# Turning a gate chain's rows between the halves of a step's scores in an mLSTM mixer

## The chip, the cores and the metric

The kernel runs on one core of one Trainium2 chip. The metric is device microseconds of one execution; the time before is the median of three runs.

## The reference, cut to what matters

A decoder block on x of shape (8, 256, 256): a Mamba layer with its MLP, an mLSTM cross mixer, and a feed-forward network with fp4 rounding. The change touches the mixer alone. Its part of the reference, for each batch b of 8 and each of 4 heads (width 64):

```python
log_fg = jax.nn.log_sigmoid(fg)
cs = jnp.cumsum(log_fg, axis=2)
log_D = cs - cs_shift.T + ig.T            # lower triangle, else -inf
max_log_D = jnp.max(log_D, axis=-1, keepdims=True)
D = jnp.exp(log_D - max_log_D)
qk = einsum(q, k) / sqrt(64)
C = qk * D
normaliser = maximum(abs(sum(C)), exp(-max_log_D))
h = einsum(C / (normaliser + 1e-8), v)
h_norm = (h - mean(h)) / sqrt(var(h) + 1e-5) * (1 + out_w)
```

The kernel writes log_D as a(t) minus a running maximum R(s), with a = ig minus the running sum of log_fg. It needs for each token a (the exponent's bias) and exp(-(cs + R)), called nm, which bounds the normaliser. It also needs R as a row, cut into three bf16 pieces that add up to it.

## The kernel before, in words

The mixer and the feed-forward network stand in one block, one program for each engine. A program is a list of stages with a lag: in step s a stage with lag g works on batch s minus g (`pipelines`, L144, and `step`, L151 onwards). Steps 0 to 11 of the mixer are written out; from step 7 on the first stages of the feed-forward network stand beside them. The order within a step is the order of the list, and each engine runs its instructions in that order. `only(n, stage)` puts a stage into step n alone.

- **TensorE**, a step: `scores1_even`, `scores0`, `scores1_odd` of batch s-1 (L1608: the products of keys and queries; keys of the second chunk with even heads, keys of the first chunk, keys of the second chunk with odd heads), then `sums` of batch s-2 (L1636 to L1638: weights times values), then `args` of batch s (L1591 to L1600: the exponents' arguments from R's pieces).
- **ScalarE**: `exps` of batch s (L1720), `squares` of batch s-2 (L1727).
- **VectorE**: `weights` of batch s-1 in two parts (L1784: scores times exponentials), `variance` of batch s-3 (L1813), `normalise` of batch s-2 (L1795 to L1806), `scale` of batch s-3 (L1818). `normalise` raises `h_read`.
- **GpSimd**: `rstds` of batch s-3 (L1878, L1880: the reciprocal root), then `residual` (L1885, L1888).
- **SyncE** loads rows of R (`load_r`, L91) and keys (`load_k`, L1567) for batches 2 to 7 in turn.

The gates' chain (`GateChain`) runs twice, for 16 rows (4 batches of 4 heads) each. The second half's runs inside the mixer's steps, one piece at a time, since batches 4 to 7 need it only from step 4 on. Its places before the change:

- step 2, VectorE, at the end: `maxima` (L399 to L411): the running maximum, then first piece, remainder, second piece, remainder, third piece, and nm's exponent cs + R. SyncE then stores the pieces (L455), and reads them back for batch 4.
- step 3, TensorE, after all of `scores`: `turn_a` (L442), two transposes of a into bank 6. VectorE, at the start of step 3: `a_tokens` (L415) copies them out and raises `gates_done` to 1.
- step 4, ScalarE, at the start: `exp_nm` (L427). TensorE, after all of `scores`: `turn_nm` (L449), into bank 7. VectorE, at the start: `nm_tokens` (L419) copies them out and raises `gates_done` to 2.

Banks 6 and 7 are the ones that `sums` writes, so the turned rows must be copied out before `sums` goes on: `sums` of batch 1 (step 3) waits for `gates_done` at 1, `sums` of batch 2 (step 4) at 2. `turn_a` waits for `h_read` of batch 0, `turn_nm` for that of batch 1, since both overwrite sums that `normalise` reads.

Of the kernel before, what the change touches and what calls it, by code (L numbers as in the profile page):

```python
# [357 lines left out]
class GateChain:  # L358
# [37 lines left out]
    def maxima(self, dve):  # L396
        at = self.SUMS_AT
        dve.wait_ge(self.dve, at)
        dve.tensor_tensor_scan(self.R, self.aT, self.aT, -3e38, ALU.max, ALU.max).then_inc(self.dve, 1)  # L399
        dve.wait_ge(self.dve, at + 1)  # L400
        dve.tensor_copy(self.pieces[:, 0, :], self.R).then_inc(self.dve, 1)
        dve.wait_ge(self.dve, at + 2)
        dve.tensor_tensor(self.rest[:, 0, :], self.R, self.pieces[:, 0, :], ALU.subtract).then_inc(self.dve, 1)
        dve.wait_ge(self.dve, at + 3)
        dve.tensor_copy(self.pieces[:, 1, :], self.rest[:, 0, :]).then_inc(self.dve, 1)
        dve.wait_ge(self.dve, at + 4)
        dve.tensor_tensor(self.rest[:, 1, :], self.rest[:, 0, :], self.pieces[:, 1, :], ALU.subtract)\
           .then_inc(self.dve, 1)
        dve.wait_ge(self.dve, at + 5)
        dve.tensor_copy(self.pieces[:, 2, :], self.rest[:, 1, :]).then_inc(self.dve, 1)  # L410
        dve.tensor_tensor(self.nm, self.cs, self.R, ALU.add).then_inc(self.dve, 1)  # L411
# [80 lines left out]
def on(stage, unit, *args, n=B):  # L492

    if 0 <= unit < n:
        stage(unit, *args)


def front(m):
# [91 lines left out]
    chain = GateChain(m, 0, lambda name, shape: (over_dead_bc if shape[0] == P else over_dead_x)(name, shape))  # L590
# [641 lines left out]
    def _(dve):  # L1232
# [50 lines left out]
        def soft_start():  # L1283
            dve.wait_ge(s["dt_ps"], 4)
            dve.tensor_tensor(raw.rearrange("p (t h) -> p t h", h=NH),
                              bank[7][:, 0:W].rearrange("p (t h) -> p t h", h=NH),
                              middle(m.head_c[:, 0, :], T), ALU.add).then_inc(s["cs_step"], 1)
            dve.wait_ge(s["cs_step"], 1)
            softplus_start(dve, s["sp_dve"], raw, work, 1.0)

        def soft_rest():
            n = softplus_finish(dve, s["sp_dve"], s["sp_act"], flat(m.dt[:]), work, 1.0)
            dve.wait_ge(s["sp_exp"], 1)
            dve.tensor_scalar(neg_a[:], neg_a[:], -1.0, None, ALU.mult).then_inc(s["sp_dve"], 1)
            dve.wait_ge(s["sp_dve"], n + 1)
            dve.tensor_tensor(m.da[:], m.dt[:], middle(neg_a[:], T), ALU.mult).then_inc(s["da_ready"], 1)

        def pieces_of_sums():
            at = 1

            def step(ins):
                nonlocal at
                at += 1
                ins.then_inc(s["cs_step"], 1)
                dve.wait_ge(s["cs_step"], at)

            turned = bank[7][:, 3 * P:4 * P]
            shifted, grid, below = work[0], work[1], work[2]
            dve.wait_ge(s["da_ps"], 1)
            dve.wait_ge(s["filled"], 1)  # L1310
            step(dve.tensor_scalar(shifted, turned, FLOOR, ON_GRID, ALU.max, ALU.add))
            step(dve.tensor_scalar(grid, shifted, ON_GRID, None, ALU.subtract))
            step(dve.scalar_tensor_tensor(below, turned, FLOOR, grid, ALU.max, ALU.subtract))
            dve.tensor_tensor_scan(both[:, 0, :], ones, grid, 0.0, ALU.mult, ALU.add)
            step(dve.tensor_tensor_scan(both[:, 1, :], ones, below, 0.0, ALU.mult, ALU.add))
            step(dve.tensor_copy(pieces[:, :, 0, :], both))
            step(dve.tensor_tensor(rest, both, pieces[:, :, 0, :], ALU.subtract))
            step(dve.tensor_copy(pieces[:, :, 1, :], rest))
            step(dve.tensor_tensor(rest, rest, pieces[:, :, 1, :], ALU.subtract))
            dve.tensor_copy(pieces[:, :, 2, :], rest).then_inc(s["pieces_ready"], 1)  # L1320
# [83 lines left out]
        def ctx_last():  # L1404
            dve.wait_ge(g["ctx_last"], 1)
            dve.wait_ge(s["later_in"], 16 * len(LATER))
            dve.tensor_tensor(m.graw[:, C * CTX_SUMS:, :], bank[7][:, 0:C * 2 * XH].rearrange("p (c g) -> p c g", c=C),
                              middle(m.gate_b[:], C), ALU.add).then_inc(g["last_saved"], 1)
# [20 lines left out]
        def quantise(b, first, end):  # L1429
            if first == 0:  # L1430
                dve.wait_ge(g["ffn_w_in"], 16)
                after(dve, g["wq_step"], Quantiser.STEPS * b)
            for k in range(first, end):
                wq.step(k, b, m.ffn_w[:, b * UNIT:(b + 1) * UNIT])

        for k in range(STEPS):
            b = k - SCAN
            on(sums, b - 3)
            if k == 6:
                soft_start()  # L1440
            on(apply, 2 * k - 2)
            on(apply, 2 * k - 1)
            on(convolve, k - 2, [0, 1])
            if k == 6:
                soft_rest()
            on(convolve, k - 2, [2, 3])
            if k == 7:
                pieces_of_sums()
            on(convolve, k - 2, [4])
            on(stats, 2 * k)  # L1450
            on(stats, 2 * k + 1)
            units = UNITS.get(k, [])
            two = len(units) == 2
            on(hidden, k - MLP, 0)
            if units:
                quantise(units[0], 0, 5 if two else 3)
            on(center_sum, 2 * (k - MLP - 2))
            on(center_sum, 2 * (k - MLP - 2) + 1)
            on(hidden, k - MLP, 1)
            on(center, 2 * (k - MLP - 2))  # L1460
            on(center, 2 * (k - MLP - 2) + 1)
            if units:
                quantise(units[0], 5 if two else 3, 9 if two else 5)
            on(inputs, b)
            on(outputs, b - 1, 0)
            on(weights, b, 0)
            on(outputs, b - 1, 1)
            on(weights, b, 1)
            if b == 4:
                ctx_last()  # L1470
            on(hidden, k - MLP, 2)
            if units:
                quantise(units[-1], 0 if two else 5, 5 if two else 7)
            on(hidden, k - MLP, 3)
            if units:
                quantise(units[-1], 5 if two else 7, 9)
            if k == MLP + 7:
                chain.logs(dve)
            on(residual, k - MLP - 1)
            if k == MLP + 7:  # L1480
                chain.sums(dve, *FIRST_HALF)
            on(gate_rows, k - MLP - 3)
            on(norm, k - MLP - 1)
            if k == MLP + 6:
                dve.wait_ge(g["gates_saved"], B // 2)
                chain.start(dve)
            if k == MLP + 7:
                chain.maxima(dve)
            if k == MLP + 8:
                chain.a_tokens(dve, TOKENS[0])  # L1490
                chain.nm_tokens(dve, TOKENS[1])
                dve.tensor_scalar(m.out_w[:], m.out_w[:], 1.0, None, ALU.add)
# [3 lines left out]
def mixer_and_ffn(m):  # L1496
# [24 lines left out]
    chain = GateChain(m, 1, lambda name, shape: sb(name, shape)[:])  # L1521
# [3 lines left out]
    for kk in range(KF):  # L1525
        w = min(P, FF - kk * P)
        at = GU_ROWS * D + kk * P
        down_groups.append(([m.ffn_w[:, at + i * FF:at + i * FF + w] for i in range(KD)], m.w_dn[0:w, kk, :]))
    saved_all = m.gu_saves + KF
    only = lambda step, stage: (lambda b, p: stage() if b == step else None, 0)  # L1530
# [54 lines left out]
    def _(pe):  # L1585
# [109 lines left out]
        def turn_nm():  # L1695
            pe.wait_ge(s["h_read"], LEAD + 2)
            chain.turn_nm(pe, TOKENS[1])

        mixer = [(scores1_even, 1), (scores0, 1), (scores1_odd, 1), only(3, turn_a), only(4, turn_nm), (sums, 2),
                 (args, 0), only(1, lambda: chain.turn_logs(pe, *SECOND_HALF))]  # L1700
        forward = [(turn_x, 2), (lambda t, p: turn_down(0 if t == 0 else 2) if round_at(t) and t < 2 else None, 2),
                   (turn_h, 4), (gate_up, 2), (lambda t, p: turn_down(1) if round_at(t) and t == 0 else None, 2),
# [4 lines left out]
    def _(act):  # L1707
# [58 lines left out]
                dst = down_groups[2 * n + half][1]  # L1766
                act.activation(dst, bank[5][0:dst.shape[0], half * D:(half + 1) * D], ACT.Copy).then_inc(m.w_saved, 1)

        mixer = [only(0, lambda: chain.exp_logs(act)), only(4, lambda: chain.exp_nm(act)), (exps, 0), (squares, 2)]
        forward = [(turned_x, 2), (lambda t, p: save_down(0 if t == 0 else 2) if round_at(t) and t < 2 else None, 2),  # L1770
                   (turned_h, 4), (lift_x, 1), (lift_h, 3), (silu, 2),
                   (lambda t, p: save_down(1) if round_at(t) and t == 0 else None, 2), (norm, 0)]
# [3 lines left out]
    def _(dve):  # L1776
# [76 lines left out]
        def output(t, p):  # L1853
# [8 lines left out]
        chain.start(dve)  # L1862
        chain.logs(dve)
        mixer = [only(3, lambda: chain.a_tokens(dve, TOKENS[0]).then_inc(m.gates_done, 1)),
                 only(4, lambda: chain.nm_tokens(dve, TOKENS[1]).then_inc(m.gates_done, 1)),
                 (lambda b, p: weights(b, p, 0), 1), (lambda b, p: weights(b, p, 1), 1), (variance, 3),
                 only(1, lambda: chain.sums(dve, *SECOND_HALF)), (normalise, 2),
# [93 lines left out]
```

## Time and profile before

| | us |
|---|---|
| median of three runs (603.13 to 605.93) | 604.32 |
| the profiled execution's own time | 606.77 |
| its span, first to last instruction | 605.1 |
| TensorE busy | 567.9 (94%) |
| VectorE busy | 446.4 (74%) |
| ScalarE busy | 270.1 (45%) |
| GpSimd busy | 144.6 (24%) |
| mean granted TensorE clock | 0.966 |

How to read it: one execution was profiled, and its times run from the first instruction. The mixer's block begins near 389.8 us; its step 3 is the stretch from about 401.7 us, step 4 from about 412.5 us, step 5 from about 419.8 us. TensorE's granted clock is given as a share of 2.4 GHz: 1.00 is 2.4 GHz, 0.50 is 1.2 GHz. PE is TensorE's matmuls, PEld its weight loads, DVE VectorE, ACT ScalarE, POOL GpSimd, SPq the issue of a DMA by SyncE. An f32 matmul shows as two records.

### The profile page before, as it was taken

Reading aid. Unit: us, or ns where it says so; the run is one execution under the profiler, and the core shown is the slowest. Engines: PE = TensorE matmul, PEld = TensorE weight load, DVE = VectorE, ACT = ScalarE, POOL = GpSimd, SP = SyncE. Lnnn points to the kernel's source line nnn. Section 1 sums busy time; section 2 is a strip of 40 time slices with the busy share of each in tenths; the row PEclk is TensorE's granted clock in tenths of the full one; section 3 lists DMA queues with packets and bytes.
Section 4 is the critical chain, followed back from the end, with each engine's and each line's share of the span. In section 5 each row is a group of like instructions: output and inputs, shape, how many; then the busy total and the mean of one; then the engine's idle time right before and its main releaser. Section 6 shows DMA issues by size and latency. Waiting matters only on the chain. (4 is left out here: it accounts for less than half of the span.)

```text
span 605.1 us, 9377 instructions
## 1 busy us (share of the span) xinstructions
PE 567.9 (94%) x2995; PEld 459.4 (76%) x2995; DVE 446.4 (74%) x990; ACT 270.1 (45%) x565; POOL 144.6 (24%) x209
## 2 busy tenths in 40 slices
PE   7989998999999899999999999989959899999995
PEld 6766666788888788888888888877855577777774
DVE  6986598379888324755655857575788999999994
ACT  2655877785788422222111112434434444444431
POOL 4120001134545021210110010005775222122200
PEclk8989999799999999999999999998977999999999
DMA  8300101000000093000000000011100000000000
GB/s 301 121 1 18 35 15 39 22 25 5 6 7 0 2 298 90 1 1 0 1 1 1 1 0 1 4 43 33 35 2 0 2 17 17 14 12 17 18 19 26
DMA packets 21392, 18.90 MB, mean 31 GB/s; under 512 B 12008, under 2 KB 20584, under 8 KB 20968
## 3 DMA queue, kind: packets, MB, share of 16 engines
q1 hardware_dynamic: 20920, 18.36, 9.5%
q8 instruction: 22, 0.36, 0.3%
q14 instruction: 18, 0.15, 0.1%
q10 hardware_dynamic: 432, 0.03, 0.1%
HBM read 16.04 MB, written 2.34 MB: 30 GB/s over the span
## 5 line engine op out<-in xcount | busy, mean ns | idle before, releaser
L923 PE MATMUL ps<-xnT,w_fc 128*128 128x256 f32 x512 | 112.8, 380 | 0.0
L923 PEld LDWEIGHTS ps<-xnT,w_fc 128*128 128x128 f32 x512 | 96.5, 190 | 12.7
L1658 PE MATMUL ps<-w_fc,scores 128*128 128x352 f32 x256 | 82.3, 476 | 1.5 <-ACT scores L1747 1.5
L1658 PEld LDWEIGHTS ps<-w_fc,scores 128*128 128x128 f32 x256 | 48.9, 196 | 29.0 <-ACT scores L1747 3.6
L1166 ACT ACTIVATE xs<-ps 128x512 f32<-128x512 f32 x32 | 19.1, 597 | 95.8 <-PE ps L923 75.7
L1279 DVE SCALAR_TENSOR_TENSOR fold<-xpad,conv_w,fold 128x256 f32<-128x256 f32 x120 | 50.9, 481 | 2.4 <-ACT fold L1068 1.6
L1677 PE MATMUL ps<-u_res,hT 128*128 128x256 f32 x192 | 44.2, 380 | 3.8 <-DVE scores L1856 2.8
L1677 PEld LDWEIGHTS ps<-u_res,hT 128*128 128x128 f32 x192 | 36.3, 190 | 11.3 <-issue 3.0
L806 PE MATMUL ps<-xnT,fold 128*128 128x256 f32 x160 | 39.2, 393 | 1.6 <-ACT xpad L1062 0.8
L806 PEld LDWEIGHTS ps<-xnT,fold 128*128 128x128 f32 x160 | 30.7, 198 | 9.5 <-issue 3.6
L813 PE MATMUL ps<-fold,xnT 128*128 128x512 f32 x64 | 36.8, 708 | 0.0
L732 POOL TENSOR_SCALAR q_ve<-q_mv 128x2 f32<-128x2 f32 x8 | 1.7, 217 | 129.3 <-DVE q_mv L1393 129.3
L898 PE MATMUL ps<-w_out,xF 128*128 128x256 f32 x128 | 30.4, 381 | 1.5 <-DVE u_res L1368 1.5
L1377 DVE TENSOR_TENSOR fold<-ps,xs 128x512 f32<-128x512 f32 x16 | 11.1, 691 | 26.2 <-ACT xs L1166 26.2
L898 PEld LDWEIGHTS ps<-w_out,xF 128*128 128x128 f32 x128 | 23.7, 190 | 8.1 <-issue 5.5
L714 POOL TENSOR_TENSOR bc<-xs,head_c 128x512 f32<-128x512 f32 x16 | 24.1, 1507 | 20.7 <-DVE zs L1361 20.7
L936 PE MATMUL ps<-zs,xpad 128*128 128x256 f32 x128 | 28.4, 380 | 0.0
L936 PE MATMUL ps<-zs,fold 128*128 128x256 f32 x128 | 28.3, 379 | 0.0
L936 PEld LDWEIGHTS ps<-zs,fold 128*128 128x128 f32 x128 | 24.3, 190 | 3.3
L936 PEld LDWEIGHTS ps<-zs,xpad 128*128 128x128 f32 x128 | 24.2, 190 | 3.3
L1377 DVE TENSOR_TENSOR xpad<-ps,xs 128x512 f32<-128x512 f32 x16 | 11.1, 692 | 20.2 <-ACT xs L1166 20.2
L1385 DVE TENSOR_TENSOR x_res<-x_res,ps 128x256 f32<-128x256 f32 x16 | 6.7, 419 | 24.2 <-PE ps L936 24.2
(299 smaller groups left out, 1208.8 us busy)
## 6 DMA issues: line engine op xcount, KB each, us to landing
zs<-in_ffn_w SPq DMA_DIRECT2D x1, 2112.0 KB, 10.9
x_res<-in_x SPq DMA_DIRECT2D x8, 256.0 KB, 7.6
w_fc<-in_w_fc SPq DMA_DIRECT2D x1, 2048.0 KB, 10.3
xnT<-in_ctxT SPq DMA_DIRECT2D x8, 256.0 KB, 3.1
xs<-in_ctx SPq DMA_DIRECT2D x16, 128.0 KB, 3.0
xs<-in_ctxT SPq DMA_DIRECT2D x8, 256.0 KB, 3.1
out<-scores SPq DMA_DIRECT2D x16, 128.0 KB, 1.7
fold<-in_w_in SPq DMA_DIRECT2D x2, 580.0 KB, 6.6
```

The lines of the kernel that those rows point to most:

```text
L714: pool.tensor_tensor(heads(dx[:, c, :]), heads(m.xs[:, n, :]), inner(m.head_c[:, 2, :], HD), ALU.mult)\
L806: last = pe.matmul(bank[1 + n % 2][:, 0:S], w_in[:, kk, w0:w0 + P], turned_u(b, kk), start=(kk == 0), stop=(kk == KD - 1))
L813: last = pe.matmul(bank[3 + c][:], turned_u(b, kk)[:, c * P:(c + 1) * P], w_in[:, kk, 0:DI], start=(kk == 0), stop=(kk == KD - 1))
L898: last = pe.matmul(bank[6][:, c * D:(c + 1) * D], ygT[:, c, k * P:(k + 1) * P], m.w_out[:, k, :], start=(k == 0), stop=(k == DI // P - 1))
L923: last = pe.matmul(bank[half + r][:, i * S:(i + 1) * S], m.w_fc1[:, kk, col:col + P], m.xnT[:, b, kk * S:(kk + 1) * S], start=(kk == 0), s ...
L936: last = pe.matmul(bank[4 + c][:, 0:D], hid[p][:, k, c * P:(c + 1) * P], w_fc2[:, k, :], start=(k == 0), stop=(k == KM - 1))
L1166: act.activation(gate[:, r, :], bank[2 + r][:], ACT.Silu).then_inc(g["gate_ready"], 1)
L1279: dve.scalar_tensor_tensor(conv[:, p, k, :], xpad[:, p, k, tap:tap + S], m.conv_w[:, ch, tap:tap + 1], conv[:, p, k, :], ALU.mult, ALU.add)\
L1377: dve.tensor_tensor(hid[p][:, 2 * pair:2 * pair + 2, :].rearrange("p k t -> p (k t)"), bank[r][:], gate[:, r, :], ALU.mult).then_inc(g["hi ...
L1385: dve.tensor_tensor(m.x_res[:, n, :], m.x_res[:, n, :], bank[4 + c][:, 0:D], ALU.add)\
L1658: last = pe.matmul(bank[1 + j][:, 0:HALF], xT[:, p, k * P:(k + 1) * P], m.w_gu[:, k, j * HALF:(j + 1) * HALF], start=(k == 0), stop=(k == ...
L1677: last = pe.matmul(bank[7][:, 0:D], hT[:, p, k, :], m.w_dn[:, k, :], start=(k == 0), stop=(k == KF - 1))
```

## The change

TensorE's two turns move ahead of `scores1_odd` of their step. `maxima` is cut after the first remainder: what follows (second piece, remainder, third piece, nm's exponent) becomes `maxima_rest`. In the second half's chain `maxima_rest` stands in step 3, right behind `a_tokens`; in the first half's it is called right behind `maxima`, as before. ScalarE's `exp_nm` moves from the start of step 4 to the start of step 3, ahead of `exps` of batch 3. No instruction is added or removed, and no wait gets another value.

```diff
@@ -401,6 +401,9 @@
         dve.tensor_copy(self.pieces[:, 0, :], self.R).then_inc(self.dve, 1)
         dve.wait_ge(self.dve, at + 2)
         dve.tensor_tensor(self.rest[:, 0, :], self.R, self.pieces[:, 0, :], ALU.subtract).then_inc(self.dve, 1)
+
+    def maxima_rest(self, dve):
+        at = self.SUMS_AT
         dve.wait_ge(self.dve, at + 3)
         dve.tensor_copy(self.pieces[:, 1, :], self.rest[:, 0, :]).then_inc(self.dve, 1)
         dve.wait_ge(self.dve, at + 4)
@@ -1486,6 +1489,7 @@
             if k == MLP + 7:
                 chain.maxima(dve)
+                chain.maxima_rest(dve)
@@ -1696,7 +1700,7 @@
-        mixer = [(scores1_even, 1), (scores0, 1), (scores1_odd, 1), only(3, turn_a), only(4, turn_nm), (sums, 2),
+        mixer = [(scores1_even, 1), (scores0, 1), only(3, turn_a), only(4, turn_nm), (scores1_odd, 1), (sums, 2),
                  (args, 0), only(1, lambda: chain.turn_logs(pe, *SECOND_HALF))]
@@ -1766,7 +1770,7 @@
-        mixer = [only(0, lambda: chain.exp_logs(act)), only(4, lambda: chain.exp_nm(act)), (exps, 0), (squares, 2)]
+        mixer = [only(0, lambda: chain.exp_logs(act)), only(3, lambda: chain.exp_nm(act)), (exps, 0), (squares, 2)]
@@ -1862,6 +1866,7 @@
         mixer = [only(3, lambda: chain.a_tokens(dve, TOKENS[0]).then_inc(m.gates_done, 1)),
+                 only(3, lambda: chain.maxima_rest(dve)),
                  only(4, lambda: chain.nm_tokens(dve, TOKENS[1]).then_inc(m.gates_done, 1)),
```

## Rows read from the trace of the kernel before

**Rows 1.** Chain of work that ended last, 384 to 458 us: start us, us, what

```profile
405.03 0.18 DVE a_tok L415
...
414.91 0.25 ACT nm L427
```

**Rows 2.** Windows: stretch, us, busy PE PEld DVE ACT POOL, granted clock, DMA, GB/s

```profile
405.35:412.50 7.15, 7.15 (x32) 5.77 (x32) 4.16 (x11) 0.71 (x2) 1.84 (x2) 0.52 0.16 43
412.50:415.94 3.44, 2.37 (x20) 2.08 (x19) 0.47 (x3) 2.65 (x9) 2.54 (x2) 1.00 0.01 2
...
419.80:442.60 22.80, 22.80 (x182) 20.22 (x181) 17.78 (x42) 12.31 (x36) 16.98 (x17) 1.00 0.09 25
442.60:454.00 11.40, 4.93 (x31) 4.32 (x30) 9.21 (x25) 3.15 (x7) 7.70 (x10) 0.68 0.01 2
```

**Rows 3.** Timeline of TensorE, steps 3 to 5: start, us, instruction, [idle before <-releaser]

```profile
401.72 2.13 PE L1608 MATMUL ps<-xnT,xs 64*128 64x128 f32 x16
403.78 0.29 PE L442 MATMUL ps<-ident,aT 16*128 16x16 f32 x2
405.35 0.41 PE L1636 MATMUL ps<-xs,zs 128*128 128x65 f32 x2 [1.28 <-DVE a_tok L415]
...
412.46 2.13 PE L1608 MATMUL ps<-xnT,xs 64*128 64x128 f32 x16
415.29 0.27 PE L449 MATMUL ps<-ident,nm 16*128 16x16 f32 x2 [0.70 <-ACT nm L427]
415.94 0.41 PE L1636 MATMUL ps<-xs,zs 128*128 128x65 f32 x2 [0.38 <-DVE nm_tok L419]
...
419.81 2.13 PE L1608 MATMUL ps<-xnT,xs 64*128 64x128 f32 x16
```

**Rows 4.** Timeline from 403.24 us: weight loads at the end of the scores

```profile
403.24 0.41 PEld L1608 LDWEIGHTS ps<-xnT,xs 64*128 64x128 f32 x3
```

**Rows 5.** Timeline of VectorE, steps 2 and 3

```profile
400.74 0.17 DVE L1795 TENSOR_SCALAR den<-ps 128x8 f32<-128x8 f32 x1 [1.38 <-PE ps L1638]
...
401.58 0.76 DVE L1806 TENSOR_TENSOR scores<-ps,den 128x256 f32<-128x256 f32 x2
...
403.27 0.41 DVE L403 TENSOR_TENSOR max_rest<-R,max_parts 16x256 f32<-16x256 f32 x1
403.72 0.28 DVE L405 CAST max_parts<-max_rest 16x256 bf16<-16x256 f32 x1
...
404.69 0.41 DVE L411 TENSOR_TENSOR nm<-cs,R 16x256 f32<-16x256 f32 x1
405.03 0.17 DVE L415 COPY a_tok<-ps 128x32 f32<-128x32 f32 x1
...
406.92 0.66 DVE L1813 TENSOR_REDUCE var<-scores 128x8 f32<-128x512 f32 x1
...
411.95 0.68 DVE L1818 TENSOR_TENSOR scores<-scores,rv 128x512 f32<-128x512 f32 x1
```

**Rows 6.** Timeline of ScalarE

```profile
403.90 0.68 ACT L1727 ACTIVATE scores<-scores 128x512 f32<-128x512 f32 x1
...
414.75 0.40 ACT L427 ACTIVATE nm<-nm 16x256 f32<-16x256 f32 x1
```

**Rows 7.** Timeline of GpSimd

```profile
408.09 1.64 POOL L1880 TENSOR_TENSOR rv<-var,minus_half 128x8 f32<-128x8 f32 x1
```

**Rows 8.** Timeline of SyncE's queue, and a DMA issue (KB, us to landing)

```profile
404.79 0.32 SPq L455 DMA_DIRECT2D running_max<-max_parts  x1
...
406.56 0.55 SPq L1567 DMA_DIRECT2D xs<-in_ctxT  x1
...
xs<-in_ctxT SPq DMA_DIRECT2D x6, 256.0 KB, 3.1
```

**Rows 9.** Timeline of TensorE: the network's first two tiles

```profile
454.14 8.03 PE L1658 MATMUL ps<-w_fc,scores 128*128 128x352 f32 x16 [1.49 <-ACT scores L1747]
...
464.33 5.00 PE L1658 MATMUL ps<-w_fc,scores 128*128 128x352 f32 x16
```

## The prediction

> **What bounds the kernel now.** The change moves work of steps 3 and 4 of the mixer, so I read those steps engine by engine. TensorE's timeline says what a step should cost: from the start of step 5's scores on, TensorE is busy without a gap, 22.80 of 22.80 us at a granted clock of 1.00 (2.4 GHz) [rows 2]. There TensorE sets the pace. Steps 3 and 4 are different. Step 3 runs from 401.72 to 412.46 (10.74 us), step 4 from 412.46 to 419.81 (7.35 us) [rows 3]. The reader is to see three things in them.
>
> First, TensorE stands idle for 1.28 us until a_tok is copied out, and only then begins batch 1's sums at 405.35 [rows 3]. The copy was late for no reason of its own: a was turned by 403.78 + 0.29 = 404.07, but VectorE was inside `maxima` until nm's exponent, started 404.69, and came to a_tok at 405.03 [rows 3, 5]. The chain that ended last passes through it [rows 1]. Second, right after that gap the granted clock falls: 0.52 on average from 405.35 to 412.50 [rows 2], that is 1.2 GHz for nearly all of it, with TensorE busy throughout. Third, in step 4 turn_nm waits 0.70 us for ScalarE's exponential of nm, which stands behind batch 3's `exps`, and the sums wait another 0.38 us for nm_tok [rows 1, 3].
>
> **The change part by part.** I follow the new order from 401.72, where nothing has changed yet.
>
> *a turned between the halves.* The last four records of the scores are the odd half. Their first weight load stands at 403.24 and the turn followed at 403.78 [rows 3, 4], so the odd half with the switch into it is about 0.45 to 0.5 us. The turn can start at about 403.3 and be done at 403.6. `h_read` of batch 0 is no hindrance: normalise starts at 400.74 and the maxima behind it are already at 403.27 [rows 5].
>
> *a copied amid the maximum's pieces.* VectorE finishes the first remainder at 403.27 + 0.41 = 403.68 [rows 5]. The copy then runs from about 403.7 to 403.9 (0.17 us for a_tok [rows 5]). From a_tok's start to the first sum it took 405.35 - 405.03 = 0.32 us [rows 3, 5], so TensorE may go on at about 404.05. It is busy with the odd half until then: 403.3, 0.29 for the turn, 0.45 for the half, so 404.1. Batch 1's sums start at 404.1 instead of 405.35: **1.25 us** saved. The bounds are 1.0 (the turn costs TensorE two switches instead of one) and 1.4.
>
> *What stands behind the copy.* The four remaining instructions of `maxima` took 405.03 - 403.72 = 1.31 us [rows 5]; behind the copy they run from about 403.85 to 405.2, against 405.10 before. So the store of the pieces goes out some 0.1 to 0.15 us later than 404.79 [rows 8], and the rows and keys of batch 4 behind it in SyncE's queue likewise: keys issued at 406.7, landed 3.1 us later at 409.8 [rows 8]. They are first read by step 5's scores, in my sum at 414.6; this costs nothing as long as that cover of 4.8 us stands. `weights` of batch 2 come at most 0.1 us later, then variance: from 406.92 to about 407.0, ended at 407.65 [rows 5].
>
> *The clock.* From 405.35 to 412.46 TensorE did batch 1's sums and batch 3's args in 7.11 us. The same two stages one step later took 419.81 - 415.94 = 3.87 us at full clock [rows 3]. The gap ahead of them is gone, so I take the clock as held: **3.2 us** saved (7.11 - 3.9), and scores of batch 3 start at 404.1 + 3.9 = 408.0 instead of 412.46. They need weights of batch 2, which are over when variance starts at 407.0, so 1 us of cover is left. Bounds of this term: 0 if it falls all the same, 3.2 if not. I take the upper end, because the stretch nearest to the new one, steps 5 to 8, holds 1.00 over 22.80 us with the same stages back to back [rows 2].
>
> *nm's exponential one step up.* nm's exponent is there at about 405.25; ScalarE ends the squares of batch 0 at 403.90 + 0.68 = 404.58 [rows 6] and then waits for it some 0.7 us, with batch 3's `exps` queued behind. Those need args of batch 3, the last part of the stretch from 404.1 to 408.0, so not before some 407. The exponential (0.40 us [rows 6]) is over at 405.7, so nothing waits for ScalarE: cost nothing, with over 1 us of cover. The 0.70 us wait of turn_nm goes.
>
> *What is late next.* turn_nm would start at 408.0 + 1.6 = 409.6, the odd half end at 410.3 to 410.35. VectorE's nm_tokens stands behind `scale` of batch 0, and this becomes a wait that before did not have. Normalise of batch 1 starts at about 407.6, now straight after variance, and takes 1.6 us (400.74 to 401.58 + 0.76 in batch 0 [rows 5]), until 409.2. GpSimd's root started 1.17 us after variance started (406.92 to 408.09) and took 1.64 us [rows 5, 7]; with variance at 407.0 it is ready at 409.8. So `scale` starts at 409.8, 0.6 us after normalise; before, it started at 411.95, long after the root was there (409.73). nm_tok follows about 0.6 us later at 410.4, and the sums 0.34 us after that as in 415.94 [rows 3], at 410.7. TensorE stands for about 0.4 us. From the start of scores to that of sums step 4 then takes 2.7 us instead of 415.94 - 412.46 = 3.48 [rows 3]: **0.75 us** saved. Bounds: 0.4 (GpSimd or VectorE half as late again) to 1.1 (no stall).
>
> *Sum.* 1.25 + 3.2 + 0.75 = 5.2 us: scores of batch 4 start near 414.6 instead of 419.81. From there TensorE sets the pace again, `residual` of batch 0 is over before batch 2's sums are, and the rest of the mixer shifts as a whole. The way from the mixer into the network runs over VectorE and GpSimd, whose order is unchanged, so the shift reaches the end. Nothing changes ahead of 403 us: the first half's instructions keep their order. Against the profiled execution's own 606.77 this gives 601.6. That execution lies 2.45 us above the median of 604.32, so I take the difference off the median: **599.1 us**.
>
> **A rule of the skill beside the row.** The granted clock was 1.00 through the 0.70 and 0.38 us gaps of step 4 and fell after the 1.28 us one [rows 2, 3]. The Trainium skill (TensorE: Matmul & The Clock Gate, What's actually happening) says that activity releases the throttle and that the same kernel shows different numbers of cold matmuls from run to run. By that rule the 3.2 us would not be in every execution before, so not surely in the median; the trace, one execution, cannot show it. It is the first rival.
>
> **The rivals.**
>
> 1. *The stall goes, the clock term does not.* Either the timed executions before mostly kept 2.4 GHz through step 3, or after the change the clock falls at another place, such as the new 0.4 us wait. For it: the three runs spread over 2.8 us, nearly the 3.2 of the term, and the profiled one is above them all. Against it: 0.52 right behind the longest gap of these steps. Gain 1.25 + 0.75 = 2.0: 602.3.
>
> 2. *More than one fall saved.* If in timed executions the step 4 gaps (0.70 + 0.38 us) also bring the clock down, both falls go, 5.2 + 3.2 = 8.4 at most: 596.0 at the lowest, some 597.5 if it holds in half of them. Against it: in this trace it did not fall there.
>
> 3. *Slower: the network's first tiles stay at 1.2 GHz.* TensorE waits at the hand-over (4.93 us busy of 11.40, clock 0.68), and the first tile's 16 products took 8.03 us against 5.00 for the second [rows 2, 9]. The change moves these waits by 5 us in time. If the clock then comes back later, each further tile costs 3.0 us; from the second further one on the gain of 5.2 is gone: 599.1 + 6 = 605.1, with a third 608.1. Against it: TensorE was back up before the second tile, and VectorE is the busier of the two at the hand-over (9.21 us of 11.40 [rows 2]), which hides part of each 3 us.
>
> 4. *It does not do what it says*: the chain behind nm_tok is longer than I think (`scale` held by GpSimd, say by 1 us more), so step 4 gains nothing. Then 1.25 + 3.2 = 4.45, less up to 0.5: about 600.2. The direction stays.
>
> **How the numbers follow.** Forecast 0.56, rival 1 0.24, rival 2 0.06, rival 3 0.04, rival 4 0.10. The range takes in the forecast's own bounds (sum of the lower bounds 1.0 + 3.2 + 0.4 = 4.6, of the upper 5.7: 598.6 to 599.7), rivals 1 and 4, and about 1 us by which medians of such runs differ: 597.2 to 602.8. About 0.5% (3.0 us) is what a measurement of this kernel can tell from no change. Below 601.3 lie the forecast, rivals 2 and 4 and little of rival 1: faster 0.74. Rival 1 and the mild end of rival 3: same 0.23. Slower 0.03.
>
> **What would show it.** In the profile of the changed kernel: no wait of L1636 for a_tok over 0.2 us; a clock of 1.00 over steps 3 and 4; the nm exponential directly behind the first squares; no wait of L449 for ScalarE; a wait of L1818 for GpSimd of about 0.6 us in step 3 and of L1636 for nm_tok of about 0.4 us; 12.9 us from the scores of batch 2 to those of batch 4 instead of 18.1. The prediction is wrong if the clock falls in step 3 or 4 all the same, if the timed runs before were mostly without the fall, or if the hand-over to the network takes longer than before.

## The result, and the profile after

The changed kernel takes 599.65 us (median of 13 runs, 597.5 to 602.84) against 605.64 us (13 runs, 602.42 to 608.96) for the kernel before: ratio 0.9926, 95% interval 0.99 to 0.9951, so 3.0 to 6.1 us faster. The ratio is not that of the two medians, which would be 0.9901: it gives 4.5 us, they give 6.0. The profiled execution took 597.5 us, its span is 595.8 us. The ratios of this document leave out executions that count as slow (739.67 us and above, and one of 609.86, one of 606.96 and one of 607.69 us), the medians and numbers of runs in the tables do not.

The windows of steps 3 and 4, first of the kernel before, then of the changed one (stretch, its length, busy time of PE, PEld, DVE, ACT, POOL, granted clock, DMA share, GB/s):

```profile
401.72:412.46 10.74, 9.46 (x50) 7.83 (x49) 7.58 (x21) 3.53 (x11) 1.84 (x2) 0.68 0.10 29
412.46:419.81 7.35, 6.28 (x50) 5.40 (x49) 3.59 (x11) 2.85 (x10) 3.87 (x4) 1.00 0.13 37
```

```profile
396.70:403.08 6.38, 6.38 (x50) 5.31 (x49) 6.14 (x18) 3.53 (x11) 0.26 (x2) 1.00 0.03 7
403.08:409.51 6.43, 6.43 (x51) 5.32 (x50) 4.92 (x14) 3.03 (x10) 5.31 (x5) 1.00 0.28 83
```

Each stretch runs from the scores of one batch to those of the next. TensorE is now busy for all of both steps and keeps its clock: 12.81 us instead of 18.09, **5.28 us** less. The changed kernel's timeline of TensorE answers to [rows 3]:

```profile
396.70 1.68 PE L1612 MATMUL ps<-xnT,xs 64*128 64x128 f32 x12
398.32 0.29 PE L445 MATMUL ps<-ident,aT 16*128 16x16 f32 x2
398.54 0.71 PE L1612 MATMUL ps<-xnT,xs 64*128 64x128 f32 x4
399.18 0.44 PE L1640 MATMUL ps<-xs,zs 128*128 128x65 f32 x2
...
403.08 1.68 PE L1612 MATMUL ps<-xnT,xs 64*128 64x128 f32 x12
404.70 0.29 PE L452 MATMUL ps<-ident,nm 16*128 16x16 f32 x2
404.92 0.71 PE L1612 MATMUL ps<-xnT,xs 64*128 64x128 f32 x4
405.63 0.41 PE L1640 MATMUL ps<-xs,zs 128*128 128x65 f32 x2
...
409.51 2.13 PE L1612 MATMUL ps<-xnT,xs 64*128 64x128 f32 x16
```

Twelve records of scores, the turn, four records, the sums: no row has an idle time in brackets, where before there were 1.28, 0.70 and 0.38 us. VectorE and ScalarE beside it (answering to [rows 5, 6]):

```profile
398.26 0.41 DVE L403 TENSOR_TENSOR max_rest<-R,max_parts 16x256 f32<-16x256 f32 x1
398.65 0.19 DVE L418 COPY a_tok<-ps 128x32 f32<-128x32 f32 x1
398.75 0.27 DVE L408 CAST max_parts<-max_rest 16x256 bf16<-16x256 f32 x1
...
404.69 0.69 DVE L1822 TENSOR_TENSOR scores<-scores,rv 128x512 f32<-128x512 f32 x1 [0.67 <-POOL rv L1885]
405.30 0.18 DVE L422 TENSOR_SCALAR nm_tok<-ps 128x32 f32<-128x32 f32 x1
```

```profile
400.16 0.42 ACT L430 ACTIVATE nm<-nm 16x256 f32<-16x256 f32 x1 [0.59 <-DVE nm L414]
```

The reader is to see a's copy amid the maximum's pieces, nm's exponential right behind its input, and the new wait of `scale` for GpSimd's root, with nm_tok behind it.

The two profiled spans differ by 9.3 us, and that is not all the change's. Scores of batch 2 start 5.02 us earlier already (401.72 against 396.70), in a part that the change does not touch, and there the clock was higher this time, 0.98 against 0.93 over the first 150 us. The windows, before and after:

```profile
0.00:150.00 150.00, 137.14 (x717) 103.26 (x717) 112.61 (x268) 98.39 (x200) 30.58 (x63) 0.93 0.18 59
```

```profile
0.00:150.00 150.00, 136.21 (x759) 105.69 (x760) 117.36 (x276) 102.05 (x207) 34.16 (x66) 0.98 0.18 59
```

From the scores of batch 4 to the end it is 605.1 - 419.81 = 185.3 us before and 595.8 - 409.51 = 186.3 us after. So 5.02 + 5.28 - 1.0 = 9.3.

The first of these three terms does not repeat: in a second profile of the changed kernel scores of batch 2 start at 401.25 us, with a clock of 0.94 over the first 150 us. The last one can be placed. From the scores of batch 4 to the first tile's products of the network it takes 34.33 us before and after, from there to the fifth tile's 36.12 us in both, and from there to the last tile's 93.02 us in both. The 1.0 us stand behind that, in one of the last groups of products, behind a wait of 2.8 us. Before, then after:

```profile
594.33 2.83 PE L1677 MATMUL ps<-u_res,hT 128*128 128x256 f32 x12 [2.83 <-DVE scores L1856]
```

```profile
584.04 4.51 PE L1681 MATMUL ps<-u_res,hT 128*128 128x256 f32 x12 [2.84 <-DVE scores L1860]
```

The granted clock over this stretch was 1.00 before and 0.61 after. Of the eleven profiles of this document nine have the slow group (4.37 to 5.46 us), among them all four with the whole change in them, and two have not: the kernel before and the one with all gaps filled. The instructions there are the same in all of them. What the kernel before does there in other executions is not shown.

### The profile page after: what moved, and what is told of

It reads as the page before. It is cut to its first block and busy times, and to the rows that moved or that the text cites. A ratio compares the mean times of both kernels' runs of the same rounds, so it can differ in the third digit from the quotient of the medians.

```text
span 595.8 us, 9377 instructions
## 1 busy us (share of the span) xinstructions
PE 563.0 (94%) x2995; PEld 457.9 (77%) x2995; DVE 446.2 (75%) x990; ACT 270.1 (45%) x565; POOL 145.7 (24%) x209
## 5 line engine op out<-in xcount | busy, mean ns | idle before, releaser
L1681 PE MATMUL ps<-u_res,hT 128*128 128x256 f32 x192 | 45.9, 391 | 3.8 <-DVE scores L1860 2.8
L1681 PEld LDWEIGHTS ps<-u_res,hT 128*128 128x128 f32 x192 | 37.5, 196 | 11.8 <-issue 3.0
L809 PE MATMUL ps<-xnT,fold 128*128 128x256 f32 x160 | 37.7, 381 | 1.4 <-ACT xpad L1065 0.9
L809 PEld LDWEIGHTS ps<-xnT,fold 128*128 128x128 f32 x160 | 29.5, 190 | 8.4 <-issue 3.0
L816 PE MATMUL ps<-fold,xnT 128*128 128x512 f32 x64 | 31.6, 621 | 0.0
## 6 DMA issues: line engine op xcount, KB each, us to landing
w_fc<-in_w_fc SPq DMA_DIRECT2D x1, 2048.0 KB, 10.3
```

The costliest lines, as they stand in the source:

```text
L809: last = pe.matmul(bank[1 + n % 2][:, 0:S], w_in[:, kk, w0:w0 + P], turned_u(b, kk), start=(kk == 0), stop=(kk == KD - 1))
L816: last = pe.matmul(bank[3 + c][:], turned_u(b, kk)[:, c * P:(c + 1) * P], w_in[:, kk, 0:DI], start=(kk == 0), stop=(kk == KD - 1))
L1681: last = pe.matmul(bank[7][:, 0:D], hT[:, p, k, :], m.w_dn[:, k, :], start=(k == 0), stop=(k == KF - 1))
```

## The experiments

Each kernel was timed in 9 to 12 runs beside the kernel before, on the same chip, and profiled once. "Stretch" is from the scores of batch 2 to those of batch 4, which is 18.09 us in the profile before and 12.81 in the one after. The 605.64 us of the first row belongs to the result above. The runs of the kernel before that the ratios go by had a median of 605.29 us for the first four variants, 604.38 for the next four, and 604.59 for the last.

| kernel | step 3 + step 4 = stretch, us | clock in them | median us | ratio to before, 95% |
|---|---|---|---|---|
| before (profile above) | 10.74 + 7.35 = 18.09 | 0.68, 1.00 | 605.64 | 1 |
| a's part alone | 6.37 + 11.31 = 17.68 | 1.00, 0.66 | 605.35 | 1.0002 (0.9974 to 1.0031) |
| nm's part alone | 10.50 + 6.63 = 17.13 | 0.70, 0.96 | 605.11 | 0.9991 (0.9958 to 1.0024) |
| a's gap filled with work | 7.50 + 9.04 = 16.54 | 1.00, 0.85 | 603.96 | 0.9977 (0.9938 to 1.0015) |
| change without the cut | 10.79 + 6.38 = 17.17 | 0.68, 1.00 | 600.82 | 0.9933 (0.9897 to 0.9969) |
| the same again | 7.50 + 6.38 = 13.88 | 1.00, 1.00 | 605.08 | 0.9996 (0.9956 to 1.0036) |
| all gaps filled with work | 7.51 + 7.70 = 15.21 | 1.00, 1.00 | 602.17 | 0.9961 (0.9936 to 0.9986) |
| the change again | 6.39 + 6.42 = 12.81 | 1.00, 1.00 | 600.83 | 0.9927 (0.99 to 0.9953) |
| nm's copy ahead of `scale` | 6.38 + 6.38 = 12.76 | 1.00, 1.00 | 599.85 | 0.9931 (0.9901 to 0.9961) |
| hand-over filled with work | 6.38 + 6.43 = 12.81 | 1.00, 1.00 | 600.89 | 0.9932 (0.9906 to 0.9959) |

### a's part alone

```diff
-        mixer = [(scores1_even, 1), (scores0, 1), (scores1_odd, 1), only(3, turn_a), only(4, turn_nm), (sums, 2),
+        mixer = [(scores1_even, 1), (scores0, 1), only(3, turn_a), (scores1_odd, 1), only(4, turn_nm), (sums, 2),
...
+                 only(3, lambda: chain.maxima_rest(dve)),
```

> Edit: a's part alone (maximum cut in two around the copy of a, a turned ahead of the odd half); nm's exponential and turn stay where they were. Theory: the stall goes (1.25 us) and with it the fall of the clock behind it (3.2 us), so scores of batch 2 to scores of batch 4 take 18.1 - 4.4 = 13.6 to 13.7 us, and the granted clock over them is 1.00; time about 4.4 us below the kernel before where that kernel lost its clock, 1.25 where it did not. Rival (the fall does not hang on this gap): 16.8 us and a clock near 0.5 somewhere in the stretch.

Step 3 came out as forecast (6.37 us, no gap). But the stretch is 17.68 us, and in time nothing is gained. The fall had moved to step 4:

```profile
404.82 2.13 PE L1612 MATMUL ps<-xnT,xs 64*128 64x128 f32 x16
408.08 0.26 PE L452 MATMUL ps<-ident,nm 16*128 16x16 f32 x2 [1.13 <-ACT nm L430]
408.72 0.66 PE L1640 MATMUL ps<-xs,zs 128*128 128x65 f32 x2 [0.38 <-DVE nm_tok L422]
...
416.13 3.38 PE L1612 MATMUL ps<-xnT,xs 64*128 64x128 f32 x16
```

With a fast step 3, TensorE comes to nm's turn earlier in relation to ScalarE, so the wait for the exponential is 1.13 us instead of 0.70; with 0.38 behind it these are gaps of 1.51 us in a row, and behind them the sums' rows take 0.66 and 0.63 us and start every 0.43 us, where at the full clock they start every 0.22 us. The clock stays down into the next scores (3.38 us instead of 2.13), so step 5 takes 7.22 us and not 5.96. Steps 3 to 5 together are thus 24.90 us, where the kernel before has 18.09 + 5.96 = 24.05. My own expectation and its rival were both off: the fall does hang on the gap, but on whichever gap is there.

### nm's part alone

```diff
-        mixer = [(scores1_even, 1), (scores0, 1), (scores1_odd, 1), only(3, turn_a), only(4, turn_nm), (sums, 2),
+        mixer = [(scores1_even, 1), (scores0, 1), only(4, turn_nm), (scores1_odd, 1), only(3, turn_a), (sums, 2),
...
-        mixer = [only(0, lambda: chain.exp_logs(act)), only(4, lambda: chain.exp_nm(act)), (exps, 0), (squares, 2)]
+        mixer = [only(0, lambda: chain.exp_logs(act)), only(3, lambda: chain.exp_nm(act)), (exps, 0), (squares, 2)]
```

> Edit: nm's part alone (exponential one step up, nm turned ahead of the odd half); a's turn and copy as before. Theory: the 1.28 us stall at a_tok stays, the clock falls behind it as before; in step 4 the waits for the exponential and nm_tok (0.70 and 0.38 us) go, scale no longer stands late because step 3 is slow, so step 4 takes about 6.2 to 6.3 us instead of 7.35. The stretch from scores of batch 2 to scores of batch 4 is about 17.0 us if the clock falls, 13.8 if it does not. Rival (the gaps of step 4 are what matters): over 2 us gained.

17.13 us against an expected 17.0, with the 1.28 us gap and the low clock in step 3 (0.70), which here reached into the start of step 4 (0.96 over it). What nm's part gives by itself is 18.09 - 17.13 = 0.96 us, which cannot be told from nothing in time.

### a's gap filled with work

```diff
             chain.turn_a(pe, TOKENS[0])
+            for _ in range(10):
+                pe.transpose(bank[7][:, 0:P], m.ident[:], m.ident[:])
```

> Edit: the kernel before with ten 128x128 transposes of the identity behind a's turn, into the bank whose contents nobody reads then; they fill TensorE's wait for a_tok (1.28 us) with about 1.1 us of work and nothing else is changed. Theory (the idle gap brings the clock down): first sum of batch 1 still about 3.6 us after the start of the step's scores, clock 1.00 behind it, sums and args of batch 1 and 3 in 3.9 us instead of 7.1; the stretch to scores of batch 4 is about 14.9 us instead of 18.1. Rival (the clock falls for another reason, for example at that distance from something earlier): still 7.1 us and 18.1 us.

```profile
403.85 0.29 PE L442 MATMUL ps<-ident,aT 16*128 16x16 f32 x2
404.08 1.31 PE L1695 MATMUL ps<-ident 128*128 128x128 f32 x10
...
409.30 2.13 PE L1608 MATMUL ps<-xnT,xs 64*128 64x128 f32 x16
412.55 0.26 PE L449 MATMUL ps<-ident,nm 16*128 16x16 f32 x2 [1.12 <-ACT nm L427]
```

Here the stall is as long as ever and only TensorE's idleness is taken away. Step 3 takes 7.50 us instead of 10.74, 3.24 us less: this is the clock by itself, and it is the 3.2 us of the prediction. That speaks for the idle gap as what brings the clock down, and against the distance from something earlier. One profile does not show it, since the next kernel keeps its clock behind a gap in one of two profiles; the count over all profiles, at the end of this section, does more. The stretch missed its expectation (16.54, not 14.9) for the reason found with a's part: nm's wait grew to 1.12 us and the fall came in step 4 (0.85, 9.04 us). In time 0.9977 (0.9938 to 1.0015) cannot be told from no change.

### The whole change but for the cut in the maximum, twice

```diff
-        mixer = [(scores1_even, 1), (scores0, 1), (scores1_odd, 1), only(3, turn_a), only(4, turn_nm), (sums, 2),
+        mixer = [(scores1_even, 1), (scores0, 1), only(3, turn_a), only(4, turn_nm), (scores1_odd, 1), (sums, 2),
...
-        mixer = [only(0, lambda: chain.exp_logs(act)), only(4, lambda: chain.exp_nm(act)), (exps, 0), (squares, 2)]
+        mixer = [only(0, lambda: chain.exp_logs(act)), only(3, lambda: chain.exp_nm(act)), (exps, 0), (squares, 2)]
```

> Edit: the whole change but for the cut in the maximum: a is turned between the halves, but copied only behind all of the maximum's pieces. Theory: a_tok is as late as before (VectorE), TensorE waits about 1.2 us for it although a was turned 0.5 us earlier, and the clock falls behind the gap: like the run with nm's part alone, stretch about 17.0 us with a fall. Rival (the turn's place is what counts): the stretch is near 12.8 us.

> The whole change but for the cut in the maximum, once more: its profile had lost the clock behind a 1.08 us gap and 17.2 us in the stretch, while its twelve timed runs lay 4 us below the kernel before. Theory: a gap of 1.08 us brings the clock down in some executions and not in others, so its times are spread over two groups, near 598 and near 605, as in the first runs. Rival (the first runs were chance and it is as slow as with nm's part alone): most runs at 604 to 606.

In both profiles TensorE waits 1.08 us for a_tok, though a was turned earlier. From the scores' start to batch 1's sums it is 3.63 us, as in the kernel before: the turn's place gives nothing while VectorE is in the maximum. First the rows of the first profile, then of the second:

```profile
399.62:410.41 10.79, 9.71 (x50) 8.04 (x49) 7.35 (x21) 3.71 (x12) 1.84 (x2) 0.68 0.10 29
...
403.25 0.64 PE L1636 MATMUL ps<-xs,zs 128*128 128x65 f32 x2 [1.08 <-DVE a_tok L415]
```

```profile
397.65:405.15 7.50, 6.42 (x50) 5.31 (x49) 6.53 (x19) 3.53 (x11) 1.33 (x2) 1.00 0.14 39
...
401.28 0.41 PE L1636 MATMUL ps<-xs,zs 128*128 128x65 f32 x2 [1.08 <-DVE a_tok L415]
```

The same kernel, the same gap, once with the fall behind it and once without: 10.79 and 7.50 us for the same work, 3.29 us apart. The times agree with that: 23 runs of it (without the one of 739.67 us) spread over 10.3 us, 12 of them from 597.4 to 602.6 us and 11 from 604.2 to 607.7, where the 13 runs of the changed kernel spread over 5.3 us. So the first twelve gave a median of 600.82 us and the next 605.08. That the two groups of times are the two cases of the profiles is likely, not shown: each kernel's time also moves by what the clock does in its first 150 us. A kernel that leaves such a gap draws its time anew in each execution, and a dozen runs do not settle its median to better than about 4 us.

### All gaps filled with work

```diff
             chain.turn_a(pe, TOKENS[0])
+            for _ in range(10):
+                pe.transpose(bank[7][:, 0:P], m.ident[:], m.ident[:])
...
             pe.wait_ge(s["h_read"], LEAD + 2)
+            for _ in range(8):
+                pe.transpose(bank[7][:, P:2 * P], m.ident[:], m.ident[:])
             chain.turn_nm(pe, TOKENS[1])
+            for _ in range(3):
+                pe.transpose(bank[6][:, P:2 * P], m.ident[:], m.ident[:])
```

> Edit: the kernel before with dummy transposes in all its waits of steps 3 and 4: ten behind a's turn, eight ahead of nm's turn, three behind it. Every stall stays as long as it was; TensorE is only kept at work in it. Theory: what the change gives is two things, the stalls (2.0 us) and the clock that either of them can bring down (up to 3.2 us, in step 3 or, where only step 3 is mended, in step 4). Here the clock stays 1.00 through both steps and the stretch from scores of batch 2 to those of batch 4 is 14.9 to 15.4 us; over many runs the time lies between the kernel before and the change, about 2 us above the change. Rival (the clock in these steps has no part in the timed difference): time as before, 605.

```profile
398.60:406.11 7.51, 7.47 (x61) 6.47 (x60) 6.54 (x19) 3.12 (x10) 1.33 (x2) 1.00 0.14 41
406.11:413.81 7.70, 7.69 (x61) 6.55 (x60) 4.65 (x13) 3.26 (x11) 4.38 (x5) 1.00 0.12 35
```

This parts the gain in two. No stall is mended, and still the kernel is faster than before: 0.9961 (0.9936 to 0.9986), 2.4 us (0.8 to 3.9), which is the clock's part over twelve runs. The profiles give 18.09 - 15.21 = 2.88 us for it, well inside. That is less than 3.24, because step 4 now takes 7.70 us instead of 7.35: once step 3 is fast, the wait for nm is longer, as with a's part alone (1.13 us) and a's gap filled (1.12 us). 15.21 - 12.81 = 2.4 us is what the stalls are worth with the clock held. In time the change lies 0.9961 - 0.9926 = 0.0035 below, 2.1 us; by the medians of runs on the same chip it is 602.17 - 600.83 = 1.3 us, and the intervals of the two ratios overlap, so the size of this part is not settled. The rival, that the clock has no part, has fallen.

### The change again

No edit: the changed kernel itself.

> The changed kernel once more. Theory: 599 to 601 us, stretch from scores of batch 2 to those of batch 4 12.8 us and clock 1.00 over it in every profile, since no gap is left that could bring the clock down. Rival (the held clock of the first profile was chance): a fall in the stretch.

12.81 us for the stretch and 1.00 over it again, and the ratio repeats (0.9927 after 0.9926).

### nm's copy ahead of `scale`

```diff
-                 only(4, lambda: chain.nm_tokens(dve, TOKENS[1]).then_inc(m.gates_done, 1)),
                  (lambda b, p: weights(b, p, 0), 1), (lambda b, p: weights(b, p, 1), 1), (variance, 3),
                  only(1, lambda: chain.sums(dve, *SECOND_HALF)), (normalise, 2),
+                 only(3, lambda: chain.nm_tokens(dve, TOKENS[1]).then_inc(m.gates_done, 1)),
```

> Edit: the changed kernel with the copy of nm moved from the start of VectorE's step 4 to step 3, between normalise and scale, so that it no longer stands behind scale's wait for GpSimd's root. Theory: the new small stall goes: sums of batch 2 start 0.3 us earlier, so the stretch is 12.5 us instead of 12.8; in time too little to be told from the change. Rival (the root's wait only moves): scale and weights of batch 3 come later and the stretch stays 12.8.

```profile
407.86 0.71 PE L1612 MATMUL ps<-xnT,xs 64*128 64x128 f32 x4
408.50 0.43 PE L1640 MATMUL ps<-xs,zs 128*128 128x65 f32 x2
```

```profile
407.97 0.19 DVE L422 TENSOR_SCALAR nm_tok<-ps 128x32 f32<-128x32 f32 x1 [1.01 <-PE ps L452]
```

The stall went, but it had been 0.05 us, not 0.3: 12.76 instead of 12.81. With nm_tok long done (408.16) the sums follow the odd half's start after 0.64 us; in the change it is 0.71 (404.92 to 405.63). The odd half simply takes that long. The rival came true rather than the expectation of 12.5 us: VectorE now waits 1.01 us for the turn, so `scale` starts 2.05 us after the scores instead of 1.61.

### The hand-over to the network filled with work

```diff
+        def warm(times, at):
+            pe.wait_ge(s["w0_exp"], LEAD + B)
+            for _ in range(times):
+                pe.transpose(bank[at][:, 0:P], m.ident[:], m.ident[:])
...
+            if b == B - 1:
+                warm(16, 0)
             pe.wait_ge(s["h_read"], LEAD + b)
...
+            if round_at(t) and t == 0:
+                warm(30, 0)
             pe.wait_ge(f["xq_step"], LEAD + Quantiser.STEPS_AWAY * (t + 1))
...
+            if round_at(t) and t == 0:
+                warm(13, 1)
             pe.wait_ge(f["xT_ready"], LEAD + t + 1)
```

> Edit: the changed kernel with dummy transposes in TensorE's waits at the hand-over from the mixer to the network: 16 ahead of the last sums, 30 ahead of the first tile's turn, 13 ahead of its products. In every profile so far the clock fell there for 13.65 us and mostly once more behind it, so the first tile's products took 7 to 8 us and in some the second tile's 6.7 us, not 5.0. Theory: with the clock held these take 5.0 us each; VectorE and GpSimd set the pace of the hand-over itself, so the first tile's gain is hidden and only what the second one lost comes back, 0.5 to 2 us in time, 598 to 600. Rival (nothing of the hand-over hangs on TensorE, or the added work delays it): time as the change, or up to 1 us above.

First this kernel's two tiles, then those of the changed kernel:

```profile
446.65 5.00 PE L1673 MATMUL ps<-w_fc,scores 128*128 128x352 f32 x16 [0.73 <-ACT scores L1762]
...
456.69 6.67 PE L1673 MATMUL ps<-w_fc,scores 128*128 128x352 f32 x16 [2.35 <-issue]
```

```profile
443.84 7.00 PE L1662 MATMUL ps<-w_fc,scores 128*128 128x352 f32 x16 [1.49 <-ACT scores L1751]
...
453.88 6.66 PE L1662 MATMUL ps<-w_fc,scores 128*128 128x352 f32 x16 [0.92 <-ACT scores L1751]
```

The clock was held through the hand-over and the first tile's products took 5.00 us instead of 7.00. The next tile started 10.04 us after the first in both kernels (456.69 - 446.65, 453.88 - 443.84). Two us of TensorE were handed to waits for VectorE, and the time is that of the change (600.89). The rival holds: nothing of the first tile hangs on TensorE's speed. The fall in the second tile stayed, and it costs nothing either: from the first tile's products to the fifth's it takes 36.13 us here, and 36.12 us both in the changed kernel and in the kernel before, whose second tile took 5.00 us [rows 9]. The expected 0.5 to 2 us was not there to be had. None of the variants beats the change by more than the runs can tell.

### The falls counted over all profiles

In six of the eleven profiles TensorE stands idle in step 3 or 4 (before, a's part alone, nm's part alone, a's gap filled, and twice the change without the cut). Five of the six have a fall of the clock in these steps, always behind a gap. In the other five, where no row of these steps has an idle time (all gaps filled, and the four with the whole change), none has. So the gap brings the fall, but not each time; what decides between two executions with the same gap is not shown.

## Why the prediction was right, point by point

**599.1 was forecast, 599.65 measured**, inside 597.2 to 602.8. As a saving, 5.2 us was forecast and 4.5 us (3.0 to 6.1) measured. The stretch was forecast at 12.9 us and is 12.81. In the pair of profiles it saves 5.28 us, of which the slow group near the end takes back 1.0, a loss that the prediction did not have; that leaves 4.3. The mechanism is the one forecast; that the time agrees to 0.6 us is partly luck, since the median it starts from rests on three runs, and a median of thirteen lies 1.3 us higher.

- *a turned and copied*, 1.25 us: from the scores' start to batch 1's sums it is now 2.48 us (399.18 - 396.70), before 3.63 [rows 3], so 1.15 us. The odd half with the switch into it takes 0.64 us, not 0.45 to 0.5; this ate 0.1.
- *The clock*, 3.2 us: sums and args take 403.08 - 399.18 = 3.90 us against 7.11. In this pair of profiles the term is exact, and filling the gap with work alone gave 3.24 us. But it is a term of the profiled execution. In time, filling all gaps gave 2.4 us (0.8 to 3.9), which fits both a fall in every execution of the kernel before (2.88 us between the profiles) and one in most of them. So the first rival is neither shown nor excluded in part; whole, with no clock term, it has fallen. Its ground was sound: a gap of this kind does not bring the fall each time, as the two profiles of one kernel show, 10.79 and 7.50 us in step 3. The Trainium skill (TensorE: Matmul & The Clock Gate, What's actually happening) says of a kernel's start that the number of cold matmuls varies from run to run of the same kernel; these two profiles show such a variation in a kernel's middle.
- *nm*, 0.75 us: from the scores' start to the sums 405.63 - 403.08 = 2.55 us against 3.48, so 0.93. The new wait of `scale` for GpSimd was there (0.67 us, 0.6 forecast), but the step "TensorE stands for about 0.4 us" was mis-sized: it stands for 0.05 to 0.07 at most, since the odd half is longer than I took it for and covers nm_tok.
- *Nothing else pays*: the keys of batch 4 were in time, ScalarE waited 0.59 us for nm (0.7 forecast) with `exps` behind it and nothing came of it; TensorE has no gap in either step.
- *Rivals.* A second fall saved (rival 2) I had given 0.06, with the argument that in the trace the gaps of step 4 did not bring the clock down. That argument was weak: they do as soon as step 3 is mended. What that means for the edit is the largest thing that the prediction missed. I summed the parts as if each would pay by itself, 4.45 us for a's part; alone it pays nothing that can be measured. Rival 3 has its sign in the profile, the second tile at 6.66 us where before it was 5.00 [rows 9], but not its cost: the fifth tile comes 36.12 us after the first in both. The 1.0 us that the profiled execution is longer behind the mixer stands elsewhere, in the slow group near the end.

## What to carry to other kernels

A stall of TensorE costs its length and, in some executions, time at the low clock behind it (here 3.2 us for a stall of 1.28 us); two such stalls near each other have to be mended together, since the clock that one of them spares the next one can lose. To part the two, fill the wait with work that nobody reads and leave the stall: what then comes back is the clock's. And where a kernel leaves a gap of about a microsecond, look at the list of its times before trusting a median of twelve.

## What the runs showed of the hardware

TensorE's granted clock behind gaps of about the same size: 1.28 us before `sums` was followed by 1.2 GHz (rows of 0.63 us instead of 0.39) in the two profiles that had it; 1.08 us once was and once was not; 1.13 and 0.38 us on either side of a short turn were (and, at 1.12 us, in a second kernel); 0.70 and 0.38 us in the kernel before were not. Where such a wait was filled with transposes of 128x128 (ten for the 1.28 us, eight and three for step 4's), 2.4 GHz (1.00) was kept behind it, in three of three waits. A wait of 2.8 us near the end of the kernel, ahead of the same twelve matmul records in every kernel, was followed by a group of 4.37 to 5.46 us in nine profiles and of 2.83 us in two.
